# Second layer's expert down product in three float32r parts, up bias added inside the gelu

## The reference, cut to what matters

```
probs  = softmax(x @ gate_W)                     # 8 experts
keep the two best of each token, normalise their weights
for each expert e:  y_e = gelu(x @ W1[e] + b1[e]) @ W2[e] + b2[e]
moe    = sum over the token's two experts of weight * y_e
```

## Time and profile before

| what | value |
|---|---|
| time, median of 3 runs | 1759.29 us (1759.19 to 1769.43) |
| profiled execution, span from first to last instruction | 1761.3 us, mean granted clock 0.964 |
| TensorE matmul busy, whole span | 1654.4 us (94%) |
| TensorE weight loads | 1288.9 us (73%) |
| VectorE, ScalarE, GpSimd busy | 1001.3 us (57%), 584.0 us (33%), 357.7 us (20%) |
| second layer's mixture | from about 1400 us to the end |

### The profile page before, as it was taken

The page is one execution under the profiler, slowest core; times in us unless marked ns, Lnnn a source line. Parts: engine busy times, 40 slices in busy tenths (PEclk is TensorE's granted clock), DMA queues, the critical chain, the costliest instruction groups (busy, mean ns, idle before and its releaser), DMA issues. The chain is left out here.

```text
span 1761.3 us, 23423 instructions
## 1 busy us (share of the span) xinstructions
PE 1654.4 (94%) x8900; PEld 1288.9 (73%) x8900; DVE 1001.3 (57%) x1541; ACT 584.0 (33%) x1064; POOL 357.7 (20%) x327
## 2 busy tenths in 40 slices
PE   7999999999998989997999998989899999999996
PEld 3899999999995777874556565758686666666672
DVE  4569678777684634456999997574526530000014
ACT  3353454444531211012544442144346521111110
POOL 1431432233031020011454543300200010000010
PEclk9899999999999979998898988999999999999998
DMA  5232132223113568557254452150101197696860
GB/s 171 77 101 68 57 112 67 94 65 113 57 43 127 197 222 286 182 178 272 91 180 170 156 199 104 39 202 1 44 8 49 39 340 275 219 330 217 320 208 31
DMA packets 113044, 251.45 MB, mean 143 GB/s; under 512 B 14726, under 2 KB 44438, under 8 KB 108182
## 3 DMA queue, kind: packets, MB, share of 16 engines
q1 hardware_dynamic: 104352, 230.72, 37.9%
q10 hardware_dynamic: 6006, 10.62, 1.7%
q0 software_dynamic: 2560, 8.39, 1.4%
HBM read 230.95 MB, written 18.75 MB: 142 GB/s over the span
## 5 line engine op out<-in xcount | busy, mean ns | idle before, releaser
L457 PE MATMUL x_s_ps<-x_cxt,x_qs 128*128 128x400 f32 (+1 forms) x1152 | 244.5, 357 | 7.6 <-ACT x_pr L599 4.1
L1246 PEld LDWEIGHTS e_ps<-e_xg,e_w 128*128 128x128 f32 x1792 | 206.7, 192 | 33.3 <-issue 33.1
L486 PE MATMUL x_o_ps<-x_cx,x_pt 128*128 128x386 f32 (+1 forms) x1248 | 228.0, 340 | 1.0 <-DVE x_o L588 1.0
L486 PEld LDWEIGHTS x_o_ps<-x_cx,x_pt 128*128 128x128 f32 (+1 forms) x1248 | 218.1, 188 | 2.6 <-DVE x_o L588 1.2
L1246 PE MATMUL e_ps<-e_xg,e_w 128*128 128x128 f32 x1792 | 209.4, 276 | 7.2 <-issue 6.3
L457 PEld LDWEIGHTS x_s_ps<-x_cxt,x_qs 128*128 128x128 f32 x1152 | 205.8, 192 | 8.8 <-issue 4.4
L1238 PE MATMUL e_ps<-e_w,xt 128*128 128x512 f32 x352 | 160.4, 597 | 1.4 <-DMA e_w<-in_L_ffn_W 1.4
L2440 PE MATMUL x_s_ps<-x_cxt,x_qs 128*128 128x512 f32 (+1 forms) x384 | 141.3, 525 | 2.8 <-ACT x_sc L2561 1.7
L1485 DVE TENSOR_TENSOR e_y<-e_ps,e_b 128x512 f32<-128x512 f32 x20 | 13.7, 687 | 204.7 <-PE e_ps L1238 204.7
L2440 PEld LDWEIGHTS x_s_ps<-x_cxt,x_qs 128*128 128x128 f32 x384 | 67.9, 194 | 79.8 <-issue 79.0
L535 DVE TENSOR_TENSOR x_pt<-x_t_ps,x_pt 128x512 fp32r<-128x512 f32 x124 | 72.5, 587 | 90.8 <-ACT x_pt L619 90.3
(11 more groups left out here) (444 smaller groups left out, 2719.0 us busy)
## 6 DMA issues: line engine op xcount, KB each, us to landing
e_w<-in_L_ffn_W SPq DMA_DIRECT2D x16, 4096.0 KB, 16.0
x_cxt<-in_ctxT SPq DMA_DIRECT2D x8, 2401.5 KB, 9.2
x_cx<-in_ctx SPq DMA_DIRECT2D x8, 2304.0 KB
e_w<-in_L_ffn_gate_up_proj SPq DMA_DIRECT2D x8, 2048.0 KB, 8.4
x_stage<-in_ctxT SPq DMA_DIRECT2D x16, 768.0 KB, 4.5
x_stage<-in_ctx SPq DMA_DIRECT2D x16, 768.0 KB, 6.0
e_w<-in_L_ffn_down_proj SPq DMA_DIRECT2D x8, 1024.0 KB, 9.5
x<-in_ctxT SPq DMA_DIRECT2D x8, 768.0 KB, 4.3
```

What stands on the lines that cost most here:

```text
L457: last = nc.tensor.matmul(s_ps[:, n, 0:b - a], qs[:, u % 2, p, c, :], cxt[:, q, c, a:b], start=(m + c == 0), stop=(m + c == len(PARTS) + C ...
L486: last = nc.tensor.matmul(o_ps[:, 0:WIDE], pt[0:rows, p, t, :], cx[0:rows, q, t, :], start=(t + m == 0), stop=(t + m == KT - 1 + len(PARTS ...
L1246: last = nc.tensor.matmul(u_ps[:, g % 2, a * PER + n, :], w1[:, e % PAIR, m, a * hidden + c * P:a * hidden + (c + 1) * P], xg[:, m, :], st ...
```

## The change

Only the second layer's mixture changes. (1) In fresh turns the down product takes three float32r products for each chunk: high h by high W2, low h by high W2, high h by low W2. ScalarE makes the gelu in place in PSUM, casts it to the high part `hs[0]`, and casts each W2 chunk to its high part; VectorE subtracts to get both low parts. The W2 parts lie in a ring of four slots (`SLOTS`), each freed by `w2_used`. The wait for W2's DMA moves from TensorE (ahead of down 0) to ScalarE (ahead of the first gelu), which also waits for the previous turn's last down product. (2) In second turns VectorE only copies `ur_ps`, TensorE transposes at once, and ScalarE makes the gelu of the transposed values, 16 instructions of 128x64 with the bias b1, straight into `h`; VectorE's copies into `h` go, and `turn_rows` moves behind the first half of the down product. (3) The `b1_rows` tile and its two broadcast DMAs for each expert go. (4) In the last expert's fresh turn `add_rows` moves behind `take`. New tiles lie over others that are no longer used.

```diff
     def load_down(self, sp, e):
         sp.dma_start(self.b1[:, e % PAIR, :], self.up_b[e]).then_inc(self.b1_in[e % PAIR], 16)
-        if self.b1_rows is not None:
-            for half in range(2):
-                sp.dma_start(self.b1_rows[half * S:(half + 1) * S, e % PAIR, :, :], bcast(self.up_rows[e, half], S)
-                             ).then_inc(self.rows_in[e % PAIR], 16)
...
+    PARTS = ((0, 0), (1, 0), (0, 1))
+    SLOTS = 4
...
+        def down_part(c, part):
+
+            n = 2 * (c % SLOTS) + part
+            return w2s[:, n, :] if n < 2 * SLOTS - 1 else w2s_end[:, :]
...
+                def down_parts(e, t, g):
+                    pe.wait_ge(hl_ready, e * NG + (g + 1))
+                    for c in range(g * PER, (g + 1) * PER):
+                        pe.wait_ge(w2l_ready, e * HC + (c + 1))
+                        for p, q in PARTS:
+                            last = nc.tensor.matmul(y_ps, hs[p][:, c, :], down_part(c, q),
+                                                    start=(c == 0 and p + q == 0), stop=(c == HC - 1 and q == 1))
+                        if c < HC - 1:
+                            last.then_inc(w2_used, 1)
+                    return last
...
-                    pe.wait_ge(w2_in[e % PAIR], (e // PAIR + 1) * 16)
                     for g in range(NG):
-                        pe.wait_ge(h_ready, t * NG + (g + 1))
-                        last = down(e, g)
+                        last = down_parts(e, t, g)
...
                     for p in range(2):
-                        pe.wait_ge(smooth, n * 2 + (p + 1))
+                        pe.wait_ge(added, n * 2 + (p + 1))
                         for c in range(KC):
                             last = nc.tensor.transpose(ht_ps[:, p, c * P:(c + 1) * P], hr[:, p, c * P:(c + 1) * P], core.ident[:, :])
                         last.then_inc(turned, 1)
-                        if p == 0:
+                    pe.wait_ge(y_ready, t)
+                    for p in range(2):
+                        if p == 1:
                             pe.wait_ge(x_in, (t + 1) * 16)
                             turn_rows()
-                    pe.wait_ge(y_ready, t)
-                    for p in range(2):
-                        pe.wait_ge(h_ready, t * NG + (p + 1) * (NG // 2))
                         for c in range(KC):
+                            pe.wait_ge(smooth, n * 2 * KC + (p * KC + c + 1))
...
-                        V.tensor_tensor(hr[:, p, :], ur_ps[:, p, :], weights.b1_rows[:, e % PAIR, p, :], ALU.add).then_inc(added, 1)
+                        V.tensor_copy(hr[:, p, :], ur_ps[:, p, :]).then_inc(added, 1)
...
-                    for p in range(2):
-                        dve.wait_ge(turned, n * 2 + (p + 1))
-                        V.tensor_copy(h[:, p * KC:(p + 1) * KC, :], ht_ps[:, p, :].rearrange("p (c n) -> p c n", n=P)).then_inc(h_ready, NG // 2)
...
                 def fresh_turn(e, t):
                     if e == FINAL:
                         first_hot()
+                    for g in range(NG):
+                        part = slice(g * PER, (g + 1) * PER)
+                        if g == 0:
+                            for c in range(PER):
+                                weight_low(e, c)
+                        dve.wait_ge(hh_ready, e * NG + (g + 1))
+                        V.tensor_tensor(hs[1][:, part, :], u_ps[:, g % 2, :, :], hs[0][:, part, :].bitcast(F32),
+                                        ALU.subtract).then_inc(hl_ready, 1)
+                        if g:
+                            for c in range(g * PER, (g + 1) * PER):
+                                weight_low(e, c)
+                    take(t + 1, e)
+                    if e == FINAL:
                         dve.wait_ge(half_ready, 2 * TT)
                         add_rows()
-                    take(t + 1, e)
+
+                def weight_low(e, c):
+                    dve.wait_ge(w2h_ready, e * HC + (c + 1))
+                    V.tensor_tensor(down_part(c, 1), w2[:, e % PAIR, c, :], down_part(c, 0).bitcast(F32),
+                                    ALU.subtract).then_inc(w2l_ready, 1)
...
+                def weight_high(e, c):
+                    if c >= SLOTS:
+                        act.wait_ge(w2_used, e * (HC - 1) + (c - SLOTS + 1))
+                    nc.scalar.copy(down_part(c, 0), w2[:, e % PAIR, c, :]).then_inc(w2h_ready, 1)
+
                 def fresh_turn(e, t, row):
                     if e:
                         act.wait_ge(x_ready, t + 1)
                         load_rows(row + BLOCKS)
                     act.wait_ge(b1_in[e % PAIR], (e // PAIR + 1) * 16)
+                    act.wait_ge(w2_in[e % PAIR], (e // PAIR + 1) * 16)
+                    if e:
+                        act.wait_ge(down_ready, t)
+                    for c in range(PER):
+                        weight_high(e, c)
                     for g in range(NG):
+                        part = slice(g * PER, (g + 1) * PER)
                         act.wait_ge(up_ready, t * NG + (g + 1))
                         for n in range(PER):
                             c = g * PER + n
-                            last = nc.scalar.activation(h[:, c, :], u_ps[:, g % 2, n, :], ACT.Gelu, bias=b1[:, e % PAIR, c:c + 1])
+                            last = nc.scalar.activation(u_ps[:, g % 2, n, :], u_ps[:, g % 2, n, :], ACT.Gelu, bias=b1[:, e % PAIR, c:c + 1])
                         last.then_inc(h_ready, 1)
+                        act.wait_ge(h_ready, e * NG + (g + 1))
+                        nc.scalar.copy(hs[0][:, part, :], u_ps[:, g % 2, :, :]).then_inc(hh_ready, 1)
+                        if g:
+                            for c in range(g * PER, (g + 1) * PER):
+                                weight_high(e, c)
...
-                        act.wait_ge(added, n * 2 + (p + 1))
-                        nc.scalar.activation(hr[:, p, :], hr[:, p, :], ACT.Gelu).then_inc(smooth, 1)
+                        act.wait_ge(turned, n * 2 + (p + 1))
+                        for c in range(KC):
+                            for half in range(2):
+                                chunk = (2 * p + half) * KC + c
+                                last = nc.scalar.activation(h[:, p * KC + c, half * S:(half + 1) * S], ht_ps[:, p, c * P + half * S:c * P + (half + 1) * S],
+                                                            ACT.Gelu, bias=b1[:, e % PAIR, chunk:chunk + 1])
+                            last.then_inc(smooth, 1)
```

More of the change, by code:

```diff
@@ L44, in sb, with over @@
         return ctx.enter_context(self.nc.sbuf_tensor(name, list(shape), dt, side=side))
+    def over(self, name, shape, dt, offset):
+        return self.nc.alloc_sbuf_tensor_at(name, list(shape), dt, offset=offset)
     def pb(self, ctx, name, shape, dt=F32):
@@ L945, with __init__ @@
 class ExpertWeights:
-    def __init__(self, core, ctx, name, up_w, up_b, down_w, down_b, up_rows=None):
-        self.up_w, self.up_b, self.down_w, self.down_b, self.up_rows = up_w, up_b, down_w, down_b, up_rows
+    def __init__(self, core, ctx, name, up_w, up_b, down_w, down_b, keep):
+        self.up_w, self.up_b, self.down_w, self.down_b = up_w, up_b, down_w, down_b
         self.w1 = core.sb(ctx, f"{name}_w1", [P, PAIR, KC, up_w.shape[2]])
@@ L952, in __init__ @@
         self.b1 = core.sb(ctx, f"{name}_b1", [P, PAIR, up_b.shape[2]])
-        self.keep = up_rows is None
+        self.keep = keep
         self.b2 = core.sb(ctx, f"{name}_b2", [P, EXPERTS if self.keep else PAIR, D])
-        self.b1_rows = core.sb(ctx, f"{name}_b1_rows", [P, PAIR, 2, 512]) if up_rows is not None else None
-        c_in0, c_in1, w1_in0, w1_in1, w2_in0, w2_in1, b1_in0, b1_in1, rows_in0, rows_in1 = core.sems(
-            ctx, f"{name}w", "c_in0 c_in1 w1_in0 w1_in1 w2_in0 w2_in1 b1_in0 b1_in1 rows_in0 rows_in1")
+        c_in0, c_in1, w1_in0, w1_in1, w2_in0, w2_in1, b1_in0, b1_in1 = core.sems(
+            ctx, f"{name}w", "c_in0 c_in1 w1_in0 w1_in1 w2_in0 w2_in1 b1_in0 b1_in1")
         self.c_in = (c_in0, c_in1)
-        self.w1_in, self.w2_in, self.b1_in, self.rows_in = (w1_in0, w1_in1), (w2_in0, w2_in1), (b1_in0, b1_in1), (rows_in0, rows_in1)
+        self.w1_in, self.w2_in, self.b1_in = (w1_in0, w1_in1), (w2_in0, w2_in1), (b1_in0, b1_in1)
     def load_biases(self, sp):
@@ L990, in __init__ @@
         self.w = w
+        self.ws_at = core.nc.sbuf_base
         self.ws = core.sb(ctx, "m1_ws", [P, KC, D])
+        self.rows_at = core.nc.sbuf_base
         self.rows = core.sb(ctx, "m1_rows", [P, 3, D])
@@ L1016, in experts @@
     w1, w2, b1 = weights.w1, weights.w2, weights.b1
[L1017 removed]
+    w1_in, w2_in, b1_in = weights.w1_in, weights.w2_in, weights.b1_in
     UPS = w1.shape[3] // hidden
@@ L1056, in experts @@
         tmp = core.sb(ctx, f"{name}_tmp", [P, 4, PER, P]) if gated else None
-        hr = None if gated else core.sb(ctx, f"{name}_hr", [P, 2, 512])
+        if not gated:
+            w2s_at = nc.sbuf_base
```

(7 more changed lines are left out.)

8 lines of the change are left out of this document (3 added, 5 removed).

## The result

The changed kernel takes 1785.05 us, median of 4 runs (1775.69 to 1795.01), beside 1762.65 us for the kernel before on the same chip (4 runs, 1759.19 to 1769.43): ratio 1.0103, 95% interval 1.0063 to 1.0143. It is slower by 1.0%, where I had forecast 1742 us. The profiled execution has a span of 1773.9 us.

The account below looks back on a forecast made before the run. TensorE was taken to bound the stage. Gains of 11.4 + 4.2 - 2.0 + 3.6 = 17.2 us took the 1761.3 us span to 1744.1; with the median 2.0 below the span, 1742 us, range 1735 to 1753.

Parts of the forecast that it names:

- The new turn with its gap lasts 28.73 - 2.85 + 1.28 = 27.16 us: Fresh turns behind fresh ones: old turn less 2.85 us of products, plus an unchanged 1.28 us of TensorE issue.
- Products: Fresh turns' down product: 48 float32r products at 0.227 us take 10.9 us, not 13.75, saving 2.85 us in each turn.
- Turns behind fresh ones: Experts 3, 5, 6, 7: casts and gelus stay hidden, so each gains the full 2.85 us, 11.4 us together.
- hidden with 1.0 us to spare: Down 0 behind fresh turns: inputs ready at 6.4 us, while TensorE finishes up 0 and up 1 at 7.41.
- thin cover at the last group: Rival: each of four groups per fresh turn starts with some 0.35 us unhidden, 11 us in all, 1753 us; chance 0.2.
- W2 held as forecast: Fresh turns behind fresh ones: W2 lands 28.4 us after the turn's start, before ScalarE wants it at 28.9.
- Turns behind second ones: Experts 1, 2, 4: down 0 waits 1.1 us and xr comes late, leaving 1.4 us gain each, 4.2 together.
- Expert 0: First fresh turn: down 0 starts 3.1 us later, TensorE idles 4.5 us, half clock costs 1.7 us; net 2.0 us loss.
- Second turns: Four second turns gain 3.6 us: 1.8 in the first, 0.4 in each of two, 1.0 in the last.
- The slow rival: Waits ahead of each chunk hold back weight loads, 0.35 us per chunk, 45 us in all, 1787 us; chance 0.05.
- TensorE waiting for low parts inside a group: Fresh turns' down product: named as a sign that the forecast is wrong; no size given.

Follow-up runs that it names:

- static pair: The changed kernel and the kernel before, both with turns written out for this input, without branches: 1747.42 us and 1758.75 us.
- a_static: Changed kernel with the turns written out for this input, no branches or loops between turns: 1747.42 us, 0.9907 of the kernel before.
- b_second: Changed kernel with float32 down products in all groups, keeping its second turns and dropped broadcasts: 1752.94 us, 0.9921 of the kernel before.
- b_norows: Kernel before, without the bias-row broadcasts of experts 2 to 7: 1761.53 us, 0.9962 of the kernel before.
- a_last_f32: Changed kernel with the last group (chunks 12 to 15) back to the float32 down product: 1758.25 us, 0.9971 of the kernel before.
- am_guard: Changed kernel with float32r parts in groups 1 and 2 only, plus an extra If around the second-turn loop: 1773.26 us, 0.9943 of the kernel before.
- al_guard: Changed kernel with float32r parts in groups 0 to 2, plus an extra If around the second-turn loop: 1769.62 us, 0.9948 of the kernel before.
- a_idle: Changed kernel with 28 idle transposes behind each fresh turn but the last: 1806.09 us, 1.0196 of the kernel before.
- a_guard: Changed kernel with an extra If jumping over the second-turn loop where an expert has just one second turn: 1767.88 us, 0.9987 of the kernel before.
- a_fill: Changed kernel with four float32 dummy products behind each fresh turn but the last: 1773.01 us, 1.0035 of the kernel before.

## Why the prediction was wrong

**The step that failed** is "The new turn with its gap lasts 28.73 - 2.85 + 1.28 = 27.16 us". I read 1.28 us of issue in the chain as the length of the control, carried it over, and did not ask what hid the rest. The control takes 4 to 7 us, and a queue of float32 products covered it: the 1.28 us were only what stuck out. The change took that cover in two ways: shorter records, and a last wait that passes later. I had asked of each new cast and subtraction what hides it, but not of the control, which the change doesn't touch. The sum has no term for it. The measured turn with its gap is 31.5 us at expert 6, 3.5 of it pause and 1.6 slower up products; all told control costs 33.5 us of the stage where it cost 8.1.

**Products: right, a little dear.** 0.232 us each, 0.227 forecast. The turn of expert 6 is 26.4 us without its pause and its half-clock loss (31.49 - 3.50 - 1.63), 25.9 forecast. Of the Trainium skill (TensorE: Matmul & The Clock Gate, Back-to-back issue gap) I had quoted 215.8 ns for 512 columns; the traces bear the row out and not the page.

**Turns behind fresh ones: over-sized.** The static pair is the measure: experts 3, 5 and 6 gain 1.48, 1.85 and 1.88 us, where I had 2.85. Of the missing microsecond 0.27 is the turn before itself (28.46, not 28.73), 0.24 the spacing (48 x 0.005) and 0.25 the last group, 3.03 for 2.78 in the chain; the other 0.2 is a wait at down 0 (0.22 us at expert 6, 0.61 at expert 3), which I had called hidden with 1.0 us to spare: in a_static ScalarE begins the casts 2.9 us after the turn's start, not 1.75. The thin cover at the last group, my likeliest rival, is thus real and small. Expert 7 gains nothing: 1.75 us slower in the static pair, as its last group of gelus begins 2.3 us after the last up product has ended, and TensorE waits 2.27 us ahead of down 3. W2 held as forecast: in after that of expert 6 lands 28.2 us after the turn's start (28.4 forecast).

**Turns behind second ones: right.** 0.88, 1.38 and 1.81 us, 4.1 together, 4.2 forecast; down 0 waits 1.1 to 1.5 us in a_static and 1.1 to 1.4 in after, 1.1 forecast.

**Expert 0: the wait and the half clock came, but not by the path of the forecast.** The timeline has, beside the earlier trace rows, a wait of 2.65 us where I had 4.5 in all:

```profile
1439.97 1.56 PE L1261 MATMUL e_ps<-e_w2s,e_hs 128*128 128x512 f32 x5 [2.65 <-DVE e_hs L1601]
```

A half-clock stretch follows, to 1444.5. I had casts, gelus and subtraction wait for W2, which would land 7.1 us after the turn's start. In after it landed at 1429.73, 0.3 us before the start, and ScalarE's high parts were ready at 1433.64. What was late is VectorE, with earlier work of the stage, as the chain shows:

```profile
1436.31 0.59 DVE x L1502
1436.91 1.80 DVE e_w2s L1613 x3
```

In the static pair down 0 is 1.3 us later (3.1 forecast), no half-clock stretch follows, and the turn is 1.0 us shorter where I had 2.0 longer. That the forecast of a loss fits the slower turn in after is partly luck.

**Second turns: 1.2 us for the first, 0.8 for the last, none for the middle ones** (16.26 and 16.18), by b_second against before; 3.6 forecast for all four. In the middle ones down begins 8.5 us after up (8.3 forecast, 9.13 before), but turn_rows takes 0.59 us of the path and not 0.44, and the down product 0.15 more. The gain of the first is not the new order's: b_norows, with the old order, has 16.19 us there, as xr is in time.

**The slow rival gave the right time by the wrong mechanism**: 1787, for waits inside the groups. a_last_f32 and a_static, which keep these waits in three and four groups and are fast, reject it. What the forecast named as a sign of error, TensorE waiting for low parts inside a group, did not happen beyond 0.03 us.

**What the pause adds up to.** TensorE's idle time ahead of turns is 4.9 us before and 24.4 after, 19.5 more. Seven stretches of half clock in after (the last one, at the kernel's end, stands in before too and is not counted), 27 us together, cost some 11 to 13 more, an estimate from up products of 9.04 us against 7.41. The 24.4 and the 11 to 13 are about the 33.5 us that control costs in after by the static pair. Of the 8.1 us before, 4.9 are pauses; the other 3 I have not traced one by one.

## Why the branch takes 3.4 to 6.3 us

The DMA queues of the trace show it. In the 15 profiles with branches TensorE has 68 far jumps of 1.2 us or more in this stage, and each goes with one transfer of the queue of kind "instruction", 16 KB, and ends 1.3 to 1.6 us after that transfer has ended (the transfers last 0.9 to 1.8 us). What varies is when the transfer starts. Two answers of the DMA view of the kernel before, at the jump of 1656.11: to 1659.9 the 16 engines are full with the weight load and no instruction has come, with 1.2 us more it has.

```profile
DMA packets 719, 1.47 MB, mean 388 GB/s; under 512 B 0, under 2 KB 0, under 8 KB 719
## 3 DMA queue, kind: packets, MB, share of 16 engines
q1 hardware_dynamic: 719, 1.47, 104.6%
...
DMA packets 918, 1.87 MB, mean 374 GB/s; under 512 B 11, under 2 KB 11, under 8 KB 917
## 3 DMA queue, kind: packets, MB, share of 16 engines
q1 hardware_dynamic: 917, 1.86, 100.3%
q8 instruction: 1, 0.02, 1.4%
```

And after, from 1665.00 to 1667.50 (the jump begins at 1665.05), with the engines nearly idle:

```profile
q1 hardware_dynamic: 57, 0.11, 11.5%
q8 instruction: 1, 0.02, 3.3%
```

With idle DMA engines the fetch starts 0.94 to 1.07 us after the jump (some 20 cases), with full ones 3.0 to 3.8 in two cases of three, earlier in the others; in a few cases of either kind it was under way or over when the jump came, and the jump took 1.2 to 2.5 us. Full engines alone do not decide it: with them the fetch began as early as 0.4 us after the jump. No run changed the load alone, so that the load is what delays the fetch is argued from these cases, not shown. So a far jump whose fetch starts after it lasts mostly 3.3 to 4.2 us in a quiet moment and up to 6.3 in a weight load: the kernel before had the longer control and the better cover. The Trainium skill says of this (Runtime: NRT & Kernel Launch, Instruction fetch mechanics) that a taken branch whose target lies outside the two pages held "forces a DMA fetch of the target page before execution can continue"; the traces agree, and add the price.

In am_guard 3.6 us lie once between reading the count and the next register instruction (1699.54 and 1703.16); a transfer of instructions, 1700.74 to 1701.67, stands there too, and the engine goes on 1.5 us after it. Left open: why in expert 7's turn of a_static, a_last_f32 and al_guard the semaphore of up 3 arrives 2.2 to 2.3 us after the last product of up 3 has ended, which holds ScalarE up.

## What to carry to other kernels

Where a kernel branches on data, the branch is paid on TensorE's sequencer and hidden only by products already queued, here at most 16 to 18 records: before making the last products of a turn shorter, or adding a late wait to them, work out how many microseconds stand behind the turn's last wait, and compare them with the control (4 to 7 us here). Half clock often followed the pauses of 3.0 to 3.7 us here, and cost 1.6 to 2.9 us more each time it held for a whole set of up products. When a chain shows a small "issue" piece, look up what it is the rest of.

## What the runs showed of the hardware that I had not expected

Instruction fetches that met the program's own weight load began up to 2.8 us later than those in a quiet moment (3.8 us after the jump against 1.0). TensorE's sequencer began its control at most 18 matmul records ahead of the array (16 transposes in a_idle, 18 records of 0.11 us behind second turns). A fetch can also stop products in a row, with no branch among them (1.28 us in a_guard). Useless products can shorten a kernel (a_fill: 24 us of them, 7 us less stage).
